# A recurrent gate block with routed experts: tile partitions in four contiguous quarters of 32 batches

## The chip, the cores and the metric

The kernel runs on one core of one Trainium2 chip. The metric is device time in microseconds (us), from the kernel's runs without a profiler.

## The reference, cut to what matters

`x` is 32 batches of 256 time steps of 128 float32 features. Everything below is float32.

```python
xn = layernorm(x, ln_w, ln_b)
u = xn @ Ws.T + bs + xn @ Wi.T + bi              # 16 states
h_t = tanh(h_{t-1} @ A.T + u_t)                  # over the 256 steps, all 32 batches
a = (H @ Wo.T + bo) * sigmoid(xn @ Wg.T + bg) + x
x = layernorm(x + a)
# 8 experts (128 -> 176 -> 128, gated), the two best of each token, plus a shared expert
x = layernorm(x + experts(x) + shared(x))
```

The recurrence is the part that cannot be split over time: each of the 256 steps needs the state of the step before, for 32 batches at once.

## The kernel before, in words

**Tiles.** The 256 steps are cut into 16 tiles of 16 steps. A tile holds 32 batches x 16 steps = 512 tokens, as 128 partitions with 4 tokens each. The 16 steps of a tile are four quarters (`tq`) of four steps (`q`). A partition holds the four steps of one quarter of one batch, 2 KB that lie together in HBM. Before, partition number = 4 x batch + quarter, so that one DMA with the pattern `k b tq (q d)` (lines 232 and 233) loads a tile (`load_x`, L426 to L429) or stores one (L511 to L514).

**From tokens to columns.** The normalized tile `xn` is transposed in four pieces of 128 x 128, one for each `q` (`four_transposes`, L1226 to L1230). Column `q * 128 + partition` of `xnT`, of the PSUM bank `pu` and of the state `hT` is then the token of that `q` and partition. The 32 columns of one time step are what `step_cols` (L388 to L390) returns: before, every fourth column of a block of 128, so with a stride of 16 bytes in float32.

**The recurrence.** One loop counter `n` runs over all engines' programs; step `n` is time step `n` for 0 to 255. In step `n` TensorE adds `A h` of the step before into the 32 columns of `pu` (L1342, a float32 matmul that the profile counts as two weight loads and two matmuls), then ScalarE takes tanh of these columns into `hT` (L656), and TensorE waits for it before the next step. Between two such matmuls TensorE does about one other piece of work, put there by hand by the tables `AT` (line 51), `AT_OWN` and the stages `SPARSE`: the projections of the next tile (L1368, L1371), the gate (L1358, L1361), the output (L1377, L1380), transposes (L1229), router logits (L1401), and the shared expert (L1270, L1275, L1280, L1287, L1288). Where there is little to do, `hold_clock` (L1311 to L1314) adds idle matmuls.

**Experts.** A tile's tokens are scattered by GpSimd (L567) into pages of 256 rows per expert in HBM (`xs`). From step 250 on, pages are loaded by SyncE (SP; L477 for rows, L482 for weights), put through the experts and scattered back by GpSimd (L574) to `ys`. The page phase ends at about 500 us of the profiled execution.

**The final sums.** For each tile, SP loads 512 KB of `ys` (L508), VectorE and, for tiles 6 to 15, TensorE (L1328 to L1330) add the parts, VectorE takes the moments (L779, L785, L793), GpSimd the root (L555), VectorE the shift (L800), ScalarE normalizes (L615), and SP stores the tile (L514). Tiles 0 to 5 are summed within the page phase. `SUM_AT` and `SUM_LAST` (lines 211 to 214) fix the order: for tiles 6 to 15 the steps are 3 apart, the load of a tile comes 5 steps before its sum and its store 9 steps after. So on SP's queue the store of tile i stands just ahead of the load of tile i + 5: store 6, load 11, store 7, load 12, and so on to store 10, load 15, and then stores 11 to 15. There are five buffers for these loads and three for the results.

**SP's queue at the start.** `load_x(0)`, four small weights (L433), `load_x(1)`, three more weights (L437), `load_x(2)`, nine small ones (L441 to L443), `load_x(3)`, `load_x(4)`. Then SP waits for `weights_zeroed` (L446), which VectorE's `other_weights` gives (L749 to L755), and issues 14 loads of expert weights (L449 to L455). VectorE's `expert_biases` (L768) waits for these at step 10, and the output gate of tile 0 (`og`, step 19) is behind it on VectorE. `other_weights` stands on VectorE behind the moments of tiles 0 to 2 (L779) and the shift of tile 2 (L800), for which GpSimd's root (L555) stands behind its `constants` (L534).

**Later loads of x** are issued 56 steps ahead of a tile's first step and used 44 steps ahead of it.

Of the kernel before, what the change touches and what calls it, by code (L numbers as in the profile page):

```python
# [6 lines left out]
def rnn_gate_moe_block(nc, x, Ws, bs, Wi, bi, Wo, bo, Wg, bg, ln_w, ln_b, A,  # L7
# [4 lines left out]
    B, S, D = x.shape  # L12
    N = A.shape[0]
    E, _, H = w1.shape
    P = 128
    STEPS = 16
    TOK = B * STEPS
    Q = TOK // P
    TILES = S // STEPS
# [53 lines left out]
    NX, NW, NH, NY, NT, NE, NL, NG, NS, NP, NB = 10, 7, 3, 5, 5, 8, 5, 3, 3, 3, 4  # L73
# [155 lines left out]
                found += [(b, i) for i in range(2 * Q * len(tiles)) if n == first + int(i / rate)]  # L229
        return found  # L230

    xv = x.rearrange("b (k tq q) d -> k b tq (q d)", tq=STEPS // Q, q=Q)
    ov = out.rearrange("b (k tq q) d -> k b tq (q d)", tq=STEPS // Q, q=Q)

    with ExitStack() as ctx:
        def sb(name, shape, dt=fp32):
# [39 lines left out]
        xt = [sb(f"xt{i}", [P, Q, D]) for i in range(NT)]  # L276
# [56 lines left out]
        yo, yn = xt[0:4], [xt[4], xn, x1r[0]]  # L333
# [19 lines left out]
        x_loaded = [sem(f"x_loaded{i}") for i in range(NT)]  # L353
# [25 lines left out]
        out_stored = [sem(f"out_stored{i}") for i in range(3)]  # L379
# [4 lines left out]
        def wait(eng, s, v):  # L384
            if v > 0:
                eng.wait_ge(s, v)

        def step_cols(t):  # L388
            tq, q = divmod(t, Q)
            return slice(q * P + tq, (q + 1) * P, STEPS // Q)  # L390

        def x1_rows(k, c):
            first = (k % NE) * 2 * Q + c * Q
# [28 lines left out]
        def _(sp):  # L422
# [3 lines left out]
            def load_x(k):  # L426
                if k >= NT:
                    sp.wait_ge(v_ready, k - NT + 1)
                sp.dma_start(xt[k % NT][:, :, :].rearrange("p q d -> p (q d)"), xv[k]).then_inc(x_loaded[k % NT], 16)  # L429

            load_x(0)
            for dst, src in ((ws_t, Ws), (wi_t, Wi), (a_t, A), (wg_t, Wg)):
# [52 lines left out]
            for n in range(BEGIN, END):  # L485
                k = event("load", n)
                if k is not None and k >= NT:
                    load_x(k)
                if n == 14:
                    sp.wait_ge(biases_ready, 1)  # L490
                    sp.wait_ge(weights_loaded, 16 * 14)
                    sp.dma_start(packed.rearrange("e p f -> p e f"), weights[:, 0:E, :]).then_inc(packed_stored, 16)
                    sp.wait_ge(pad_made, 3)
                    sp.dma_start(xs[E * STRIDE:E * STRIDE + PAGE, :].rearrange("(p h) f -> p (h f)", h=HALF),
                                 pad[:, :, :].rearrange("p h f -> p (h f)")).then_inc(pad_stored, 16)
                if n == PAD_AT:
                    pads()
                for _, j, c in [load for load in loads if load[0] == n]:
                    load_page(j, c)
                k = summed(n, "load")  # L500
                if k is not None:
                    if k in (0, SOON):
                        for i in range(NY):
                            last = max(j for j in range(sum(PAGES) if k else EARLY_PAGES) if j % NY == i)
                            sp.wait_ge(y_scattered[i], page_done(last))
                    wait(sp, ysum_ready, k - NL + 1)
                    wait(sp, po_ps, k - NL + 1 - SOON)
                    sp.dma_start(yl[k % NL][:, :, :, :].rearrange("p q c d -> p (q c d)"),  # L508
                                 ys[2 * TOK * k:2 * TOK * (k + 1), :].rearrange("(p r) d -> p (r d)", p=P)).then_inc(yl_loaded[k % NL], 16)
                k = summed(n, "store")  # L510
                if k is not None:  # L511
                    i = k
                    sp.wait_ge(normed["out"], i + 1)
                    sp.dma_start(ov[k], yn[i % 3][:, :, :].rearrange("p q d -> p (q d)")).then_inc(out_stored[i % 3], 16)  # L514
                k = event("second", n)
                if k is not None:
                    sp.wait_ge(normed["mid"], k + 1)
                    sp.dma_start(x1_rows(k, 1), x1_rows(k, 0)).then_inc(second_copied[k % NE], 16)
                    if k >= APART:
                        sp.dma_start(yb[k][:, HALF:Q, :], x1_rows(k, 0)[:, HALF:Q, :]).then_inc(half_kept[k % NE], 16)  # L520
            for i in range(3):
                sp.wait_ge(out_stored[i], 16 * len(range(i, TILES, 3)))

        @block.gpsimd
        def _(g):
# [78 lines left out]
        def _(act):  # L604
# [44 lines left out]
            for n in range(BEGIN, END):  # L649
                if n == at("xnT_out", 0):  # L650
                    act.wait_ge(state_weights_ready, 1)
                if 0 <= n < STEPS * TILES:
                    k, t = divmod(n, STEPS)
                    c = step_cols(t)
                    act.wait_ge(h_ps, n + 1)
                    nc.scalar.activation(hT[k % 2][0:N, c], pu[k % 2][0:N, c], ACT.Tanh, bias=bu[:, 0:1]).then_inc(h_ready, 1)  # L656
                for q in range(Q):
                    k = event("in_norm", n, q)
                    if k is not None:
                        wait(act, xnT_ps, k)  # L660
                        normalize("in", k, lambda q: xt[k % NT][:, q, :], xn, (q,))
                for h in range(2):
                    cols = slice(h * PAGE, (h + 1) * PAGE)
                    k = event("xnT_out", n, h)
                    if k is not None:
                        act.wait_ge(xnT_ps, k + 1)
                        ins = nc.scalar.activation(xnT[k % 2][:, cols], pm[:, cols], ACT.Identity, scale=lnw, bias=lnb)
                        if h:
                            ins.then_inc(xnT_ready, 1)
                    k = event("gate_out", n, h)  # L670
                    if k is not None:
                        act.wait_ge(gate_ps, k + 1)
                        wait(act, og_ready, k - NG + 1)
                        ins = nc.scalar.activation(gth[k % NG][:, cols], pm[:, cols], ACT.Tanh, scale=0.5, bias=bgh[:, 0:1])
                        if h:
                            ins.then_inc(gate_ready, 1)
                    k = event("x1T_out", n, h)
                    if k is not None:
                        act.wait_ge(x1T_ps, k + 1)
                        if k >= NS and h == 0:  # L680
                            act.wait_ge(lg_ps, k - NS + 1)
                            act.wait_ge(wb_ps, SHARED_UNIT[k - NS, 0] + 1)
                        ins = nc.scalar.activation(x1T_half(k, h), transposer(k)[:, cols], ACT.Identity)
                        if h:
                            ins.then_inc(x1T_ready, 1)
                if n == PAD_AT + 1:
                    pads()
                b = group("tanh", n)
                if b is not None:
                    act.wait_ge(route_step, 22 * b + 2)  # L690
                    j = Q * len(GROUPS[b])
                    nc.scalar.activation(ex8["th"][:, 0:j, :], ex8["ls"][:, 0:j, :], ACT.Tanh, scale=0.125).then_inc(th_ready, 1)
                for u, j in pages_at("xT", n):
                    act.wait_ge(xpT_ps, j + 1)
                    if j >= NP:
                        act.wait_ge(wb_ps, UNIT_OF_PAGE[j - NP] + 1)
                    nc.scalar.activation(xpT[j % NP][:, :], pt[:, 0:PAGE], ACT.Identity).then_inc(xpT_ready, 1)  # L697
                for u in units_at(n, "t3a", "t3b", "silu"):
                    if SLOT[u]["t3a"] == n:
                        third_a(u)  # L700
                    if SLOT[u]["t3b"] == n:
                        third_b(u)
                    if SLOT[u]["silu"] == n:
                        silu(u)
                for h in range(2):
                    k = summed(n, f"norm{h}")
                    if k is not None:
                        i = k
                        if h == 0:
                            wait(act, out_stored[i % 3], 16 * (i // 3))  # L710
                        for q in (2 * h, 2 * h + 1):
                            normalize("out", i, lambda q: summed_rows(i, q), yn[i % 3], (q,))

        @block.vector
        def _(v):
# [384 lines left out]
            for n in range(BEGIN, END):  # L1100
# [4 lines left out]
                for h in range(2):  # L1105
                    k = event("in_stats", n, h)
                    if k is not None:
                        v.wait_ge(x_loaded[k % NT], 16 * (k // NT + 1))
                        moments("in", lambda q: xt[k % NT][:, q, :], k, (h,))
                k = event("in_scale", n)  # L1110
                if k is not None:
# [5 lines left out]
                k = event("og", n)  # L1117
# [341 lines left out]
```

## Time and profile before

| | us |
|---|---|
| median of 3 runs | 537.75 (537.72 to 538.87) |
| span of the profiled execution, first to last instruction | 536.5 |
| TensorE busy | 478.4 (89%) |
| VectorE busy | 341.1 (64%) |
| ScalarE busy | 337.4 (63%) |
| GpSimd busy | 305.0 (57%) |
| mean granted TensorE clock | 0.946 |

The profiled execution's own device time is not given beside its span; the median of the unprofiled runs is 1.3 us above the span. A row of a timeline gives start, duration, engine, line, operation, tiles and how many instructions of the kind were merged. PE is TensorE's matmul, PEld its weight load, DVE VectorE, ACT ScalarE, POOL GpSimd; SPq is a DMA that SyncE issues, with the time of the issue, not of the transfer. In brackets stands how long the engine was idle before and what ended that.

### The profile page before, as it was taken

The numbers are of one execution on the slowest core, as the hardware profiler recorded it, in microseconds if no ns is written. First come the engines' busy times: TensorE is split into PE (matmuls) and PEld (weight loads), VectorE is DVE, ScalarE is ACT, GpSimd is POOL, SyncE is SP. The second block draws the span as 40 slices with busy tenths as digits, with TensorE's granted clock in tenths as the row PEclk, the third lists the DMA queues.
The fourth block names the chain that finished last, engine by engine and source line by source line (L and its number), as shares of the span: only waits on it lengthen the run. The fifth ranks groups of instructions, "written<-read, shape, count | busy, mean of one in ns | idle before, by whom it ended". The sixth has DMA issues, their size and how long they took to land.

```text
span 536.5 us, 11146 instructions
## 1 busy us (share of the span) xinstructions
PE 478.4 (89%) x2842; PEld 381.2 (71%) x2842; DVE 341.1 (64%) x1514; ACT 337.4 (63%) x870; POOL 305.0 (57%) x337
## 2 busy tenths in 40 slices
PE   5889999999999999897899857999999999999871
PEld 3657777777777777686788746988888888767530
DVE  5353579797979788746575763445454467667752
ACT  3654777777677776435567524677777777777553
POOL 4000003676766676467377777777657777885331
PEclk9977999999999999759999878899999999999987
DMA  3771112232233222278446476558657888841682
GB/s 107 151 235 56 49 47 63 88 92 87 90 90 91 89 72 74 67 220 231 122 140 188 130 215 202 156 140 246 200 167 214 228 264 270 250 167 62 225 288 78
DMA packets 58228, 79.81 MB, mean 149 GB/s; under 512 B 11182, under 2 KB 37803, under 8 KB 58166
## 3 DMA queue, kind: packets, MB, share of 16 engines
q1 hardware_dynamic: 48940, 61.64, 39.7%
q0 software_dynamic: 8640, 16.93, 9.3%
q8 instruction: 24, 0.39, 0.3%
q10 hardware_dynamic: 586, 0.53, 0.3%
q14 instruction: 38, 0.31, 0.2%
HBM read 47.85 MB, written 25.84 MB: 137 GB/s over the span
## 4 chain that ended last, share of the span: by engine, by line
PE 72%; DVE 10%; issue 5%; ACT 5%; DMA 3%; SPq 2%; ACTq 1%; POOL 1%; DVEq 0%; POOLq 0%
PE pu L1342 13%; PE py L1287 9%; PE p L1270 8%; PE py L1288 7%; PE p L1275 7%; PE ph L1280 7%; PE pt L1424 3%; PE pm L1401 3%; DMA weights<-ys 2%; PE pu L1229 2%; ACT hT L656 2%; PE pm L1358 2%; DVE z L1076 2%; PE pu L1380 1%; PE pu L1377 1%
## 5 line engine op out<-in xcount | busy, mean ns | idle before, releaser
L574 POOL DMA_INDIRECT ys<-yp,xp x142 | 141.4, 996 | 55.8 <-issue 38.4
L567 POOL DMA_INDIRECT xs<-x,place_i x128 | 124.1, 970 | 68.4 <-ACT hT L656 28.1
L656 ACT ACTIVATE hT<-pu,bu 16x32 f32<-16x32 f32 x256 | 78.6, 307 | 78.3 <-PE pu L1342 74.3
L1342 PEld LDWEIGHTS pu<-hT,aT 128*128 128x128 f32 x512 | 81.8, 200 | 58.2 <-ACT hT L656 52.8
L1342 PE MATMUL pu<-hT,aT 128*128 128x32 f32 x512 | 105.7, 293 | 11.6 <-ACT hT L656 11.5
L647 ACT ACTIVATE hid<-z 128x512 f32<-128x512 f32 x103 | 64.7, 628 | 65.3 <-DVE z L1076 63.3
L1071 DVE SCALAR_TENSOR_TENSOR z<-p,wp,t3a 128x256 f32<-128x256 f32 x71 | 34.3, 483 | 78.5 <-ACT t3a L635 68.0
L1287 PE MATMUL py<-wp,hid 128*128 128x128 f32 x284 | 60.4, 295 | 14.2 <-DVE yp L1097 12.0
L1287 PEld LDWEIGHTS py<-wp,hid 128*128 128x128 f32 x284 | 46.0, 196 | 29.8 <-DVE yp L1097 19.9
L555 POOL TENSOR_TENSOR rstd_in<-ve_in,neghalf 128x4 f32<-128x4 f32 x16 | 16.4, 1026 | 73.8 <-DVE ve_in L793 73.7
L1288 PE MATMUL py<-wp,hid 128*128 128x128 f32 x284 | 56.6, 282 | 0.0
L1288 PEld LDWEIGHTS py<-wp,hid 128*128 128x128 f32 x284 | 44.8, 199 | 0.0
L1270 PE MATMUL p<-xpT,wp 128*128 128x256 f32 x142 | 43.6, 390 | 0.0
L1275 PE MATMUL p<-xpT,wp 128*128 128x256 f32 x142 | 43.0, 385 | 0.0
L1280 PE MATMUL ph<-xpT,wp 128*128 128x256 f32 x142 | 42.6, 382 | 0.1
L635 ACT ACTIVATE t3a<-p,wp 128x256 f32<-128x256 f32 x71 | 33.3, 469 | 7.1 <-issue 4.5
L640 ACT ACTIVATE t3b<-ph,wp 48x256 f32<-48x256 f32 x71 | 33.4, 470 | 5.6 <-PE ph L1280 3.7
L1076 DVE SCALAR_TENSOR_TENSOR z<-ph,wp,t3b 48x256 f32<-48x256 f32 x71 | 33.8, 476 | 2.8 <-ACT t3b L640 2.6
L697 ACT ACTIVATE xpT<-pt 128x256 f32<-128x256 f32 x71 | 27.2, 383 | 10.1 <-PE pt L1424 8.7
L1424 PE MATMUL pt<-ident,xp 128*128 128x128 f32 x142 | 28.7, 285 | 3.9 <-issue 2.9
L615 ACT ACTIVATE xn<-xt,shift_in,rstd_in 128x128 f32<-128x128 f32 x64 | 30.3, 478 | 2.4 <-DVE shift_in L800 2.4
L555 POOL TENSOR_TENSOR rstd_out<-ve_out,neghalf 128x4 f32<-128x4 f32 x16 | 17.7, 1107 | 23.8 <-DVE ve_out L793 23.8
(264 smaller groups left out, 984.4 us busy)
## 6 DMA issues: line engine op xcount, KB each, us to landing
wp<-packed SPq DMA_DIRECT2D x71, 320.0 KB, 3.3
xp<-xs SPq DMA_DIRECT2D x71, 130.0 KB, 2.9
weights<-ys SPq DMA_DIRECT2D x16, 512.0 KB, 4.4
xt<-in_L_attn_x SPq DMA_DIRECT2D x16, 256.0 KB, 3.1
x<-x SPq DMA_DIRECT2D x16, 256.0 KB, 2.7
packed<-weights SPq DMA_DIRECT2D x1, 2560.0 KB, 8.6
ys<-yp,xp POOLq DMA_INDIRECT x142, 3.0
yb<-x SPq DMA_DIRECT2D x16, 128.0 KB, 2.8
```

The costliest lines, as they stand in the source:

```text
L567: g.indirect_dma_start(out=xs[:, :], out_offset=bass.IndirectOffsetOnAxis(ap=place_i[b % NB][:, c, t * Q + q:t * Q + q + 1], axis=0), in_= ...
L574: g.indirect_dma_start(out=ys[:, :], out_offset=bass.IndirectOffsetOnAxis(ap=xp[j % NX][:, h, DEST:DEST + 1].bitcast(int32), axis=0), in_= ...
L647: nc.scalar.activation(hid[u % NH][:, :], z[u % 2][:, :], ACT.Silu).then_inc(hid_ready, 1)
L656: nc.scalar.activation(hT[k % 2][0:N, c], pu[k % 2][0:N, c], ACT.Tanh, bias=bu[:, 0:1]).then_inc(h_ready, 1)
L1076: nc.vector.scalar_tensor_tensor(out=z[u % 2][0:REST, PAGE:2 * PAGE], in0=ph[0:REST, 0:PAGE], scalar=packed_of(u)[0:REST, BIAS + 2:BIAS + ...
L1270: nc.tensor.matmul(p3[:, 0:PAGE], w[:, W3A:W3A + P], src, start=True, stop=True).then_inc(w3_ps, 1)
L1275: nc.tensor.matmul(p1[:, 0:PAGE], w[:, W1A:W1A + P], src, start=True, stop=True).then_inc(w1_ps, 1)
L1280: nc.tensor.matmul(ph[:, 0:PAGE], w[:, WB:WB + P], src, start=True, stop=True).then_inc(wb_ps, 1)
L1287: nc.tensor.matmul(o, hid[u % NH][:, h * P:(h + 1) * P], w[:, W2A:W2A + D], start=True, stop=False)
L1288: ins = nc.tensor.matmul(o, hid[u % NH][:, PAGE + h * P:PAGE + (h + 1) * P], w[:, W2B:W2B + D], start=False, stop=True)
L1342: nc.tensor.matmul(pu[k % 2][:, step_cols(t)], aT[:, :], before, start=False, stop=True, skip_group_check=True).then_inc(h_ps, 1)
L1424: ins = nc.tensor.transpose(pt[:, h * P:(h + 1) * P], xp[j % NX][:, h, 0:D], ident[:, :])
```

## The change

A tile's partition number becomes 32 x quarter + batch. The 32 columns of a time step are then contiguous. A load of x and a store of the result become four DMAs of 32 partitions (64 KB) each, on the same semaphores, whose waits count four times as much.

```diff
-    xv = x.rearrange("b (k tq q) d -> k b tq (q d)", tq=STEPS // Q, q=Q)
-    ov = out.rearrange("b (k tq q) d -> k b tq (q d)", tq=STEPS // Q, q=Q)
+    QUARTERS = STEPS // Q
+    xv = x.rearrange("b (k tq q) d -> k tq b (q d)", tq=QUARTERS, q=Q)
+    ov = out.rearrange("b (k tq q) d -> k tq b (q d)", tq=QUARTERS, q=Q)
...
         def step_cols(t):
             tq, q = divmod(t, Q)
-            return slice(q * P + tq, (q + 1) * P, STEPS // Q)
+            return slice(q * P + tq * B, q * P + (tq + 1) * B)
...
             def load_x(k):
                 if k >= NT:
                     sp.wait_ge(v_ready, k - NT + 1)
-                sp.dma_start(xt[k % NT][:, :, :].rearrange("p q d -> p (q d)"), xv[k]).then_inc(x_loaded[k % NT], 16)
+                for tq in range(QUARTERS):
+                    sp.dma_start(xt[k % NT][tq * B:(tq + 1) * B, :, :].rearrange("p q d -> p (q d)"), xv[k, tq]).then_inc(x_loaded[k % NT], 16)
...
                     sp.wait_ge(normed["out"], i + 1)
-                    sp.dma_start(ov[k], yn[i % 3][:, :, :].rearrange("p q d -> p (q d)")).then_inc(out_stored[i % 3], 16)
+                    for tq in range(QUARTERS):
+                        sp.dma_start(ov[k, tq], yn[i % 3][tq * B:(tq + 1) * B, :, :].rearrange("p q d -> p (q d)")).then_inc(out_stored[i % 3], 16)
...
-                sp.wait_ge(out_stored[i], 16 * len(range(i, TILES, 3)))
+                sp.wait_ge(out_stored[i], 16 * QUARTERS * len(range(i, TILES, 3)))
...
-                            wait(act, out_stored[i % 3], 16 * (i // 3))
+                            wait(act, out_stored[i % 3], 16 * QUARTERS * (i // 3))
...
-                        v.wait_ge(x_loaded[k % NT], 16 * (k // NT + 1))
+                        v.wait_ge(x_loaded[k % NT], 16 * QUARTERS * (k // NT + 1))
```

## Rows read from the trace of the kernel before

**Rows 1.** Page: the chain that ended last, shares of the span by line.
```profile
PE pu L1342 13%; PE py L1287 9%; PE p L1270 8%; PE py L1288 7%; PE p L1275 7%; PE ph L1280 7%; PE pt L1424 3%; PE pm L1401 3%; DMA weights<-ys 2%; PE pu L1229 2%; ACT hT L656 2%; PE pm L1358 2%; DVE z L1076 2%; PE pu L1380 1%; PE pu L1377 1%
```

**Rows 2.** Timeline of TensorE and ScalarE, one recurrence step at full clock.
```profile
100.68 0.30 PEld L1342 LDWEIGHTS pu<-hT,aT 128*128 128x128 f32 x2 [0.31 <-ACT hT L656]
...
101.13 0.31 ACT L656 ACTIVATE hT<-pu,bu 16x32 f32<-16x32 f32 x1
...
101.50 0.30 PEld L1342 LDWEIGHTS pu<-hT,aT 128*128 128x128 f32 x2 [0.29 <-ACT hT L656]
```

**Rows 3.** Chain in order of time (start, us, what), 101 to 110 us.
```profile
101.10 0.51 PE pu L1380 x2
...
108.46 0.87 PE pm L1401 x8
```

**Rows 4.** The tanh's line L656: ns minimum/median/maximum, first and last start.
```profile
L656 ACT ACTIVATE hT<-pu,bu x256: 291/308/313, 13.1 to 250.6; 16x32 f32<-16x32 f32 x128
```

**Rows 5.** Timelines: last pair of weight loads, and the reader that waited for it.
```profile
95.54 0.30 PEld L1401 LDWEIGHTS pm<-gwT,x1T 128*128 128x128 f32 x2
...
95.98 0.19 DVE L1158 COPY lg<-pm 128x32 f32<-128x32 f32 x1 [1.29 <-PE pm L1401]
...
50.49 0.25 PEld L1229 LDWEIGHTS pu<-ident,og 128*128 128x128 f32 x2
...
51.02 0.69 DVE L1127 SCALAR_TENSOR_TENSOR x1r<-xt,pu 128x512 f32<-128x512 f32 x1 [1.50 <-PE pu L1229]
```

**Rows 6.** Groups by line and form: busy us, mean ns of one | idle before.
```profile
L674 ACT ACTIVATE gth<-pm,bgh 128x256 f32<-128x256 f32 x32 | 14.3, 448 | 0.0
...
L667 ACT ACTIVATE xnT<-pm,vcol 128x256 f32<-128x256 f32 x32 | 17.3, 543 | 1.7 <-PE pm L1229 1.7
...
L615 ACT ACTIVATE x1r<-pm,shift_out,rstd_out 128x128 f32<-128x128 f32 x3 | 1.2, 453 | 0.6 <-DVE shift_out L800 0.6
...
L902 DVE TENSOR_REDUCE new<-sel 128x8 f32<-128x64 bf16 x8 | 2.1, 266 | 0.3
...
L846 DVE TENSOR_REDUCE row_max<-lg 128x8 f32<-128x64 f32 x8 | 1.7, 212 | 0.0
```

**Rows 7.** Timeline of SP's DMA issues at the start.
```profile
3.08 0.42 SPq L433 DMA_DIRECT2D xpT<-in_L_attn_Wg  x1
...
5.49 0.54 SPq L429 DMA_DIRECT2D xt<-in_L_attn_x  x1
...
8.11 0.27 SPq L441 DMA_DIRECT2D brow<-in_L_ffn_b  x1
...
9.12 1.19 SPq L429 DMA_DIRECT2D xt<-in_L_attn_x  x2
```

**Rows 8.** Chain in order of time at the start.
```profile
0.80 3.25 DMA xt<-in_L_attn_x
...
5.78 1.04 POOL rstd_in L555
...
12.34 1.00 POOL rstd_in L555
...
17.17 0.36 SPq L449
```

**Rows 9.** Timeline of SP's DMA issues in the final sums.
```profile
509.63 0.54 SPq L508 DMA_DIRECT2D weights<-ys  x1
...
517.98 0.55 SPq L514 DMA_DIRECT2D out<-xn  x1
518.62 0.54 SPq L508 DMA_DIRECT2D weights<-ys  x1
...
528.60 0.54 SPq L514 DMA_DIRECT2D out<-x1r  x1
530.02 0.54 SPq L514 DMA_DIRECT2D out<-xt  x1
```

**Rows 10.** Chain in order of time in the final sums.
```profile
518.62 4.39 DMA weights<-ys
```

## The prediction

> **What bounds the kernel now.** I read the chain that ended last first [rows 1]. Its largest single line is L1342, the recurrence's matmul, with 13% of the span; the tanh L656, which alternates with it, is there with 2%. To see which of the two engines sets the pace I went to the timeline of one step [rows 2]. The first weight load of L1342 starts at 100.68 us, the tanh at 101.13, the next weight load at 101.50. So 0.45 us pass from TensorE to ScalarE, 0.31 in the tanh, and about 0.06 to the next load: 0.82 us a step. TensorE's other work in such a step is a pair like L1380 with 0.51 us in the chain [rows 3], and the weight loads of L1342 still wait 0.29 to 0.31 us for the tanh [rows 2]. The step is therefore bound by the round trip and not by TensorE's throughput, except where the eight small matmuls of L1401 (0.87 us, [rows 3]) stand between two steps; there TensorE is late, once in each tile. What shortens the matmul's or the tanh's latency shortens nearly every step. The page phase from about 250 us does not read the 32 columns at all.
>
> The other two places that the change touches are SP's queue at the start and in the final sums. At the start the chain goes from x over the moments and GpSimd's root (12.34 us) to the first load of expert weights (17.17 us) [rows 8]; all that follows waits for these weights. At the end SP stores a tile and only then issues the load of another: the store at 517.98 is followed by the load at 518.62 [rows 9], and that load is in the chain with 4.39 us [rows 10].
>
> **Part 1, the matmul's columns: 0.005 us a step.** No row shows L1342 with contiguous columns, so I bound it by readers that wait for a last pair of matmuls. With 8 contiguous columns (L1401) the reader starts 0.44 us after the pair's first weight load, with 128 contiguous ones (the transposes of L1229) 0.53 us [rows 5]. A straight line between them gives 0.44 + 24/120 x 0.09 = 0.46 us for 32. L1342 takes 0.45 [rows 2]. So the stride of 16 bytes costs the matmul nothing that a row at this resolution shows; at most 0.01, if 32 contiguous columns came out like 8. I take 0.005. By the Trainium skill (Advanced Engine Details and Errata, Memory Cachelines), "Any non-contiguous AP significantly slows down matmuls" where PSUM is concerned, since its lines hold two float32. By that rule this term would be the change's main gain; it gives no figure, and these rows do not agree with it at 32 columns.
>
> **Part 2, the tanh: 0.020 us a step.** It takes 308 ns for 32 strided elements [rows 4]. The same function from PSUM, also with a bias from SBUF, takes 448 ns for 256 contiguous ones (L674). The slope comes from L667 and L615, both with scale and bias: (543 - 453)/128 = 0.70 ns per element. Then 32 contiguous elements would take 448 - 224 x 0.70 = 291 ns [rows 6], 17 ns less than now. A second pair of rows, on VectorE, compares reductions of 64 elements to 8: 212 ns in order (L846), 266 ns with a stride of 16 bytes (L902) [rows 6]: 0.84 ns more for each element, which for 32 would be 27 ns. I take 20. The bounds are 0 (a short instruction may have a fixed length) and about 45 (with a slope of 0.84 ns the contiguous tanh would come to 448 - 188 = 260).
>
> **How many steps gain.** The first 21 steps lie ahead of the wait for the expert weights, and steps 240 to 255 among page work. Of the 219 between, about 14 are bound by L1401 and some 15 by other waits (ranks, VectorE). That leaves 190. Gain: 190 x 0.025 = 4.75 us. TensorE has room for it: 0.51 for the other pair and 0.22 for L1342's (two of the eight that take 0.87 us, [rows 3]) make 0.73 against a step of 0.79.
>
> **Part 3, price of a quarter transfer on SP.** A whole tile's issue takes 0.54 us, and two take 1.19 with the gaps, 0.05 between two issues. The nearest others are 0.42 us (128 rows of 512 B) and 0.27 (8 rows) [rows 7]. None has 32 rows of 2 KB. I take 0.45, as rows of 128 partitions lie on both sides of it, so with the gap 4 x 0.49 = 1.96 us in place of 0.60: 1.36 us more a tile. The bounds are 4 x 0.31 and 4 x 0.60: 0.65 and 1.8 more. By the Trainium skill (DMA: Bandwidth & Descriptors, Rules for kernel authors), two transfers to disjoint halves of the partitions run one behind the other on the same engines, and one of 128 partitions is to be preferred: it speaks against this part, and agrees with putting no gain on the shorter transfers.
>
> **Part 4, the start: +1.8 us.** Tile 2's first quarter is issued at 5.49 + 2 x 1.36 = 8.2, its last at 9.7. Landing of a whole tile took 3.25 us and the way from landing to the root 5.78 - 4.05 = 1.7 [rows 8]; with 2.8 for a quarter's landing the root of tile 2 starts at 14.2 in place of 12.34. SP itself has issued tiles 3 and 4 by 9.12 + 3 x 1.36 + 8 x 0.49 = 17.1 [rows 7], ahead of 17.17 + 1.8, so it adds nothing. Queued behind are 14 weight loads, and VectorE and the gate of tile 0 behind these: the delay goes through. Bounds +0.5 (with 0.31 a quarter only tile 0 is late) and +3.5 (0.60 and 3.25 us landing).
>
> **Part 5, loads in the scan and stores in the page phase: 0.** A load is issued 12 steps (10 us) ahead of its use, and SP is mostly idle; 1.4 us more are covered. If that cover went, each tile would pay up to 1.4. The stores of tiles 0 to 5 fall at or behind the last page loads, with SP idle again.
>
> **Part 6, the final sums: +4.8 us.** The store of tile i stands ahead of the load of tile i + 5, whose sum stands on VectorE ahead of the shift of i + 3 and so of its store: a loop of three tiles. One turn, load 12 to load 15, takes 518.62 - 509.63 = 9.0 us [rows 9]. Every turn now takes 1.36 more. Stores 7 and 10 are in two full turns: 2.7. The turn before (stores 4 and 5) has some slack: 0.5. The last store's last quarter goes out 3 x 0.49 = 1.5 later, and stores 14 and 15 are 1.42 apart [rows 9], closer than 1.96: 0.5 more. A quarter may land 0.4 sooner than a whole tile, as I took it at the start. 2.7 + 0.5 + 1.5 + 0.5 - 0.4 = 4.8. Bounds: 1.8 and 7.4 with the two prices.
>
> **Part 7, nothing.** Other places of tokens in the partitions change neither the number of rows per expert nor the count or size of scatters, pages and waits: 0. The semaphore waits are the same waits with larger numbers: 0.
>
> **Sum.** Against the profiled execution: 1.8 - 4.75 + 4.8 = +1.85 us. Its span of 536.5 stands 1.3 us below the median of the runs, and I carry the difference over: 537.75 + 1.85 = 539.6.
>
> **Rivals.**
> 1. The stride is dearer than these rows say, in the tanh, in the matmul, or both. The point from which it decides is 6.6 / 190 = 0.035 us a step. At 0.055 (45 ns of tanh, 10 of matmul) it gives 10.5 us, and 537.75 + 6.6 - 10.5 = 533.9. For it: 13% of the chain is this line. Against it: 0.45 us is what the two contiguous rows give. Chance 0.16, at 532 to 536.6. The Trainium skill's rule on PSUM lines (Advanced Engine Details and Errata, Memory Cachelines) points here.
> 2. A quarter's issue is cheap, 0.27 us. The costs are then 0.5 + 1.8, and the time 537.75 + 2.3 - 4.75 = 535.3, faster. For it: the row of 8 partitions. Against it: a 128-row issue with short rows is 0.42, so the number of rows is not the whole price. Chance 0.13.
> 3. The change does not do what it says: 32 elements are too few for the stride to matter, the tanh has a fixed length, and only SP's costs are left: 537.75 + 6.6 = 544.4. For it: the tanh's minimum of 291 ns [rows 4] occurs with the stride too. Chance 0.18.
> 4. Gain and costs are alike, within 0.2% (1.1 us), about what a measurement of this kernel can tell from no change. Chance 0.14.
>
> The forecast itself, slower at 538.9 to 544, keeps 0.39. In sum: faster 0.29, same 0.14, slower 0.57. The range from 533.8 to 544.8 leaves out 0.1 on each side; the forecast's own is 538.9 to 544.
>
> **What the changed profile would show.** The tanh's median at 285 to 292 ns in place of 308, and L1342's first load to the tanh still at 0.45 us; steps at 0.79 us. Four x issues of about 0.45 us a tile on SP, and the first load of expert weights at 19 us in place of 17.17. Four stores a tile in the final sums, with load 15 some 3.5 us further from the page phase's end, the last issue 5 us further. Wrong would prove me: a tanh at 308 or under 270, a latency well under 0.44 us in the matmul, or quarters at 0.3 us.

## The result, and the profile after

The changed kernel takes 534.6 us (median; the kernel before beside it 538.0). The ratio, taken over the fast runs alone, is 0.9934, with a 95% interval from 0.9910 to 0.9959: faster by 0.7%, or 3.6 us (2.2 to 4.8). The difference is small, but its interval leaves out 1. The forecast was slower by 1.85 us. The profiled execution went from a span of 536.5 to 531.9 us.

The page of the changed kernel, the chain that ended last by line (L1346 is the recurrence's matmul, L1342 before; lines from the load of x to SP's store are 3 higher than before, all behind the store 4 higher):

```profile
PE pu L1346 11%; PE py L1291 9%; PE p L1274 7%; PE py L1292 7%; PE p L1279 7%; PE ph L1284 7%; PE pt L1428 3%; PE pm L1405 3%; DMA weights<-ys 3%; POOL ys L578 2%; PE pu L1233 2%; PE pm L1362 2%; ACT hT L660 1%; DVE z L1080 1%; PE pu L1384 1%
```

The recurrence's matmul fell from 13 to 11% [rows 1], the loads of the final sums rose from 2 to 3%. The tanh's line, and a timeline of two steps:

```profile
L660 ACT ACTIVATE hT<-pu,bu x256: 262/278/279, 14.0 to 242.6; 16x32 f32<-16x32 f32 x128
```
```profile
100.66 0.30 PEld L1346 LDWEIGHTS pu<-hT,aT 128*128 128x128 f32 x2
...
101.11 0.28 ACT L660 ACTIVATE hT<-pu,bu 16x32 f32<-16x32 f32 x1
101.43 0.30 PEld L1346 LDWEIGHTS pu<-hT,aT 128*128 128x128 f32 x2
...
102.21 0.30 PEld L1346 LDWEIGHTS pu<-hT,aT 128*128 128x128 f32 x2
```

The tanh's median went from 308 [rows 4] to 278 ns. Two steps take 102.21 - 100.66 = 1.55 us, 0.775 each, against 0.82 [rows 2]. By the exact starts the usual distance between two tanhs went from 0.814 to 0.777 us: 37 ns, 30 of them the tanh's own. The other 7 lie between the first weight load of L1342 and the start of the tanh, 0.455 us in the median before and 0.448 after. The last tanh starts at 242.6 us in place of 250.6 [rows 4].

The start, SP's issues and the chain in order of time, and x's row of the page:

```profile
0.80 1.78 SPq L432 DMA_DIRECT2D xt<-in_L_attn_x  x4
...
4.02 0.42 SPq L436 DMA_DIRECT2D xpT<-in_L_attn_Wg  x1
...
7.51 1.70 SPq L432 DMA_DIRECT2D xt<-in_L_attn_x  x4
...
12.14 3.67 SPq L432 DMA_DIRECT2D xt<-in_L_attn_x  x8
```
```profile
4.02 2.04 DMA xpT<-in_L_attn_Wg
...
9.74 1.01 POOL rstd_in L559
...
12.81 0.99 POOL rstd_in L559
...
17.63 0.35 SPq L452
```
```profile
xt<-in_L_attn_x SPq DMA_DIRECT2D x64, 64.0 KB, 2.0
```

The root of tile 2 starts at 12.81 us (12.34 before), the first load of expert weights at 17.63 (17.17) [rows 8]: 0.46 us later.

The final sums, SP's issues (each x4 is one tile's store) and pieces of the chain:

```profile
502.49 1.72 SPq L518 DMA_DIRECT2D out<-xn  x4
504.30 0.37 SPq L511 DMA_DIRECT2D weights<-ys  x1
...
512.52 1.71 SPq L518 DMA_DIRECT2D out<-xn  x4
514.33 0.37 SPq L511 DMA_DIRECT2D weights<-ys  x1
...
525.81 2.13 SPq L518 DMA_DIRECT2D out<-xt  x4
```
```profile
494.17 4.87 DMA weights<-ys
...
504.30 4.77 DMA weights<-ys
...
514.33 4.13 DMA weights<-ys
```

The loop that the prediction describes is now in the chain with three loads (tiles 9, 12 and 15), each behind a store. A turn takes 514.33 - 504.30 = 10.0 us in place of 9.0 [rows 9].

Where the 4.6 us of the two profiled executions lie, by the starts of the first output gate, the last tanh and the first final sum on TensorE (us; the other columns are experiments, told below; the last row is called the last stretch from here on):

| stretch | before | after | columns only | quarters only | hT in step order | the same, late loads first |
|---|---|---|---|---|---|---|
| start to first output gate | 31.8 | 32.3 | 31.8 | 32.2 | 31.8 | 32.1 |
| to the last tanh | 218.7 | 210.3 | 211.8 | 214.6 | 211.7 | 214.2 |
| of it steps 48 to 240 | 162.2 | 157.0 | 157.0 | 162.3 | 157.0 | 157.0 |
| to the first final sum | 249.1 | 249.8 | 246.5 | 249.9 | 250.2 | 249.6 |
| to the end | 36.8 | 39.6 | 37.3 | 40.0 | 37.5 | 32.6 |

So +0.4, -8.4, +0.6 and +2.8. Steps 48 to 240 took 162.2 to 162.3 us in all three profiled kernels whose hT has strided columns, and 156.9 to 157.1 in all eleven in which they are contiguous; the rest of the scan does not repeat so well, because of the clock. The windows from 33 to 58 us, in the kernel before and in the changed one (busy time of the five engines, granted clock, DMA share, GB/s):

```profile
33.00:58.00 25.00, 22.93 (x120) 17.41 (x118) 11.90 (x63) 12.42 (x39) 2.25 (x4) 0.73 0.42 143
```
```profile
33.00:58.00 25.00, 22.68 (x137) 17.59 (x137) 12.93 (x67) 14.08 (x45) 2.25 (x4) 0.86 0.45 148
```

Around the wait for the expert weights TensorE was busy for 3.3, 3.7 and 2.7 of each 4 us from 24 to 36 us before, and for 3.2, 3.8 and 2.6 after. Then the clock fell to 1.2 GHz in both, at 34.6 us for 13.7 us before, and at 36.8 us for 6.8 us after (granted 0.73 and 0.86 of the stretch). Steps 24 to 48 took 24.5 and 21.9 us. Most of that difference is not the change's: with contiguous columns alone they took 24.2 us at 13.7 us of low clock. So about 2.3 of the 8.4 us are this execution's clock.

What ends the span is not the last store. The last instructions of GpSimd and of SP, before and after:

```profile
L235 POOLq DRAIN  x1: 9300/9300/9300, 526.9 to 526.9; - x1
...
L235 SPq DRAIN  x1: 13/13/13, 532.6 to 532.6; - x1
```
```profile
L237 POOLq DRAIN  x1: 9300/9300/9300, 522.4 to 522.4; - x1
...
L237 SPq DRAIN  x1: 7/7/7, 529.4 to 529.4; - x1
```

GpSimd's program ends with a drain that begins with its last root (that of tile 15) and takes 9.30 us. The span ends 0.2 us behind it, 9.50 us from the start of that root. SP, which waits for the landing of the last store, was done 3.6 us earlier before and 2.2 us earlier after. The chain of the profile does not show this: it breaks off at ScalarE's last normalization.

### The profile page after: what moved, and what is told of

The parts are those of the page before. It is cut to its first block, busy times and chain, and to the rows that moved or that the text cites. A ratio compares the mean times of both kernels' runs of the same rounds, so it can differ in the third digit from the quotient of the medians.

```text
span 531.9 us, 11242 instructions
## 1 busy us (share of the span) xinstructions
PE 469.5 (88%) x2842; PEld 379.6 (71%) x2842; DVE 341.1 (64%) x1514; ACT 334.2 (63%) x870; POOL 308.8 (58%) x337
## 4 chain that ended last, share of the span: by engine, by line
PE 67%; DVE 10%; issue 6%; ACT 5%; DMA 4%; SPq 3%; POOL 3%; ACTq 1%; DVEq 0%; POOLq 0%
PE pu L1346 11%; PE py L1291 9%; PE p L1274 7%; PE py L1292 7%; PE p L1279 7%; PE ph L1284 7%; PE pt L1428 3%; PE pm L1405 3%; DMA weights<-ys 3%; POOL ys L578 2%; PE pu L1233 2%; PE pm L1362 2%; ACT hT L660 1%; DVE z L1080 1%; PE pu L1384 1%
## 5 line engine op out<-in xcount | busy, mean ns | idle before, releaser
L578 POOL DMA_INDIRECT ys<-yp,xp x142 | 145.2, 1023 | 55.6 <-issue 36.9
L660 ACT ACTIVATE hT<-pu,bu 16x32 f32<-16x32 f32 x256 | 70.8, 277 | 73.0 <-PE pu L1346 64.0
L1346 PEld LDWEIGHTS pu<-hT,aT 128*128 128x128 f32 x512 | 81.0, 196 | 49.8 <-ACT hT L660 40.9
L1346 PE MATMUL pu<-hT,aT 128*128 128x32 f32 x512 | 101.8, 282 | 10.8 <-ACT hT L660 10.3
L701 ACT ACTIVATE xpT<-pt 128x256 f32<-128x256 f32 x71 | 27.2, 383 | 10.2 <-PE pt L1428 8.8
```

The costliest lines, as they stand in the source:

```text
L578: g.indirect_dma_start(out=ys[:, :], out_offset=bass.IndirectOffsetOnAxis(ap=xp[j % NX][:, h, DEST:DEST + 1].bitcast(int32), axis=0), in_= ...
L1346: nc.tensor.matmul(pu[k % 2][:, step_cols(t)], aT[:, :], before, start=False, stop=True, skip_group_check=True).then_inc(h_ps, 1)
```

## The experiments

**Contiguous columns alone**, on the kernel before:

```diff
-            return slice(q * P + tq, (q + 1) * P, STEPS // Q)
+            return slice(q * P + tq * B, q * P + (tq + 1) * B)
```

> The kernel before with contiguous columns in step_cols alone; x and the result still move in one transfer a tile with the old partition order. So the recurrence joins tokens that do not belong together; every instruction and its size stays. Theory A (two separate effects: columns pay, the quarters on SP's queue cost): tanh 278 ns, steps of 0.777 us in place of 0.814, and since nothing is added on SP, about 8 us faster than before: 530 us, ratio 0.985. Rival B (the gain comes from the new order of tokens or the shorter transfers, the columns only from the tanh's 0.020 us that I forecast): steps 0.79, ratio 0.991 to 0.993 like the changed kernel's.

Measured: 530.6 us, ratio 0.9869 (0.9825 to 0.9914). The tanh is at 278 ns, the step at 0.777. Theory A: the columns are worth 1.3%, 7 us (4.6 to 9.4), more than the whole change. The interval of the ratio just reaches rival B's 0.991; what decides is the step, 0.777 and not 0.79.

**The quarters alone**, the changed kernel with the reverse of that diff:

> The changed kernel with the strided columns put back in step_cols; the recurrence again joins tokens that do not belong together. Theory A: steps of 0.814 us again, SP's quarters at both ends cost 3.5 us: 541.5 us, ratio 1.0065. Rival B (transfers of a quarter land sooner, 2.0 in place of 3.1 us, and cost nothing in sum): ratio 1.000 within 0.2%.

Measured: 541.4 us, ratio 1.0077 (1.0045 to 1.0110). The quarters cost 4.1 us (2.4 to 5.9), against 6.6 in the prediction. Together the two effects give 0.9869 x 1.0077 = 0.9945, and the change measured 0.9934. Rival B of this run, no cost in sum, falls too.

**Which memory's stride costs**, the changed kernel with strided columns on one side only (`strided_cols` is `step_cols` as it was before). For SBUF:

```diff
-                    before = hT[k % 2 if t else 1 - k % 2][:, step_cols((t - 1) % STEPS)]
+                    before = hT[k % 2 if t else 1 - k % 2][:, strided_cols((t - 1) % STEPS)]
...
-                    nc.scalar.activation(hT[k % 2][0:N, c], pu[k % 2][0:N, c], ACT.Tanh, bias=bu[:, 0:1])
+                    nc.scalar.activation(hT[k % 2][0:N, strided_cols(t)], pu[k % 2][0:N, c], ACT.Tanh, bias=bu[:, 0:1])
```

> The changed kernel, but the tanh writes its 32 states to strided columns of hT in SBUF, and the recurrence's matmul reads them strided; PSUM is contiguous for both engines. The output projection then joins tokens that do not belong together. Theory A1 (the tanh's 30 ns are PSUM reads of lines that are used for one element): tanh 278 ns, and first weight load to tanh 0.45 us; Theory A2 (SBUF's strided write is what costs the tanh): tanh 308 ns. Rival B (a short tanh's length depends on both): between.

For PSUM:

```diff
-                    nc.tensor.matmul(pu[k % 2][:, step_cols(t)], aT[:, :], before,
+                    nc.tensor.matmul(pu[k % 2][:, strided_cols(t)], aT[:, :], before,
...
-                    nc.scalar.activation(hT[k % 2][0:N, c], pu[k % 2][0:N, c], ACT.Tanh, bias=bu[:, 0:1])
+                    nc.scalar.activation(hT[k % 2][0:N, c], pu[k % 2][0:N, strided_cols(t)], ACT.Tanh, bias=bu[:, 0:1])
```

> The mirror of the one before: the recurrence's matmul writes, and the tanh reads, strided columns of PSUM; hT in SBUF is contiguous for both. The recurrence joins tokens that do not belong together. Theory A1: tanh 308 ns, last weight load to tanh 346 ns (matmul slower by 7 ns), steps 0.814 us. Theory A2: tanh 278 ns and matmul as in the changed kernel, steps 0.777 us.

The tanh's line, first with SBUF strided, then with PSUM strided:

```profile
L664 ACT ACTIVATE hT<-pu,bu x256: 292/308/313, 13.4 to 252.1; 16x32 f32<-16x32 f32 x128
```
```profile
L664 ACT ACTIVATE hT<-pu,bu x256: 262/278/279, 13.5 to 243.7; 16x32 f32<-16x32 f32 x128
```

With SBUF strided the scan is as before the change: 308 ns, 0.814 us a step, steps 48 to 240 in 162.2 us; one run took 541.9 us (the quarters alone: 541.4). With PSUM strided it is as after it: 278 ns, 0.777, 157.0 us; one run took 536.0 us (the changed kernel: 534.6). The 30 ns are the tanh's strided write to SBUF. The other 7 ns belong to the matmul (first weight load to tanh 0.456 us with SBUF strided, 0.449 with PSUM strided) and go with hT too, which it reads; its PSUM write is ruled out. Theory A2.

**hT in step order, everything else as before.** If PSUM's stride is free, the partitions need not be reordered at all. On the kernel before:

```diff
+        def hT_cols(t):
+            tq, q = divmod(t, Q)
+            return slice(q * P + tq * B, q * P + (tq + 1) * B)
+
+        def by_step(t, lo, hi):
+            return t[:, lo:hi].rearrange("d (q b tq) -> d q tq b", q=(hi - lo) // P, tq=STEPS // Q)
...
-                    nc.scalar.activation(hT[k % 2][0:N, c], pu[k % 2][0:N, c], ACT.Tanh, bias=bu[:, 0:1]).then_inc(h_ready, 1)
+                    nc.scalar.activation(hT[k % 2][0:N, hT_cols(t)], pu[k % 2][0:N, c], ACT.Tanh, bias=bu[:, 0:1]).then_inc(h_ready, 1)
...
-                    before = hT[k % 2 if t else 1 - k % 2][:, step_cols((t - 1) % STEPS)]
+                    before = hT[k % 2 if t else 1 - k % 2][:, hT_cols((t - 1) % STEPS)]
...
-                    nc.tensor.matmul(pu[k % 2][:, 0:PAGE], woT[:, :], hT[k % 2][:, 0:PAGE], start=True, stop=True)
+                    nc.tensor.matmul(by_step(pu[k % 2], 0, PAGE), woT[:, :], hT[k % 2][:, 0:PAGE], start=True, stop=True)
```

(and the same for the second half, and for the zeroed first state).

> The old partition order with its single transfers. Only hT in SBUF is in time-step order: the tanh writes, and the recurrence's matmul reads, contiguous columns there, while PSUM keeps the strided columns for both; the output projection L1377/L1380 writes its 256 columns to PSUM in permuted order, so the output gate sees the old order again. All values are the reference's. Theory A2 (all of the gain is SBUF's contiguous columns, PSUM's stride is free at any size here): steps 0.777 us, L1377/L1380 as long as before (0.51 us a pair in the chain), and nothing on SP, so as the contiguous columns alone: 530 to 531 us, ratio 0.987. Rival B (a permuted PSUM write of 256 columns is slowed, as 32 columns are too few to show it): L1377/L1380 at 0.9 us a pair or more, twice a tile, 16 tiles: up to 13 us slower than A2, ratio 1.00 to 1.01.

Measured: 531.1 us, ratio 0.9875 (0.9840 to 0.9910). It has the full gain of the columns and no cost on SP. The chain of this kernel has the projection with its 256 permuted columns at the time of the contiguous one [rows 3]:

```profile
111.40 0.51 PE pu L1384 x2
```

**One transfer a tile in the changed layout:**

```diff
-                for tq in range(QUARTERS):
-                    sp.dma_start(xt[k % NT][tq * B:(tq + 1) * B, :, :].rearrange("p q d -> p (q d)"), xv[k, tq]).then_inc(x_loaded[k % NT], 16)
+                sp.dma_start(xt[k % NT][:, :, :].rearrange("p q d -> p (q d)"), xv[k]).then_inc(x_loaded[k % NT], 16)
```

and the same for the store.

> The changed kernel with one transfer a tile for x and for the result, the four quarters as the outermost dimension of the pattern in HBM. Theory A (a transfer is spread over as many DMA engines as its outermost dimension allows, here four): landing of x at 6 us or more in place of 3.1, the result's likewise, so that the start is later by 5 us or more and the end by 3: 540 us or more. Rival B (it is spread over the 128 partitions as before): landing 3.1 us, and 530 us.

Measured: 544.7 us in one run, theory A. The start of its chain, a late piece of it, and the loads' row of its page:

```profile
0.80 5.79 DMA xt<-in_L_attn_x
...
518.40 8.08 DMA weights<-ys
```
```profile
weights<-ys SPq DMA_DIRECT2D x16, 512.0 KB, 7.0
```

The first x takes 5.79 us in place of 3.25 [rows 8]. In the final sums the 512 KB loads, whose own pattern is unchanged, take 7.0 us in the median and 8.08 at the end, behind the slow stores. I had expected the start 5 us later and the end 3. The first load of expert weights went out at 19.7 us in place of 17.2, only 2.5 later, and the last stretch is 47.5 us, 10.7 more than before. Of these, 7.7 lie ahead of GpSimd's last root; the other 3.0 come behind it, as here alone of all the profiled kernels the stores landed after GpSimd's drain (SP was done at 542.7 us, the drain at 539.7). The size fits a transfer spread over few DMA engines, but no row shows how many. By the Trainium skill (DMA: Bandwidth & Descriptors, Why a DMA increments its semaphore by 16 and not by 1), a transfer runs on the largest number of engines, at most 16, that divides the slowest dimension of both patterns, here 4; the slower landing agrees. That is why the change moves quarters in four transfers.

**The order of SP's queue.** First all loads of tiles 6 to 15 two steps earlier, ahead of the stores:

```diff
-    SUM_LAST = dict(load=-5,
+    SUM_LAST = dict(load=-7,
```

on the kernel with hT in step order and on the changed kernel.

> The one before, and in the final sums the load of tile i + 5 goes on SP's queue two steps earlier, ahead of the store of tile i. Theory A (the final sums' loop of three tiles runs over SP's order, store ahead of load): the loads no longer wait for ScalarE, TensorE's and VectorE's waits for them (9 us in the kernel before) go, and the 36.8 us from the first final sum to the end shrink by 3 to 6: 525 to 528 us. Rival B (the loads are bound by their own transfers, 4.4 us for 512 KB, which then queue behind each other): within 1 us of the one before.

> The changed kernel with the load of tile i + 5 two steps earlier, ahead of the store of tile i. Theory A (the quarters cost through the loop store, load, sum, store): most of the 3 us that the final sums lost come back, with what the order costs anyhow: the stretch from the first final sum to the end 34 to 36 us in place of 39.6; 529 to 531 us. Rival B (SP's issue time itself is the bound, 1.9 us a store): 38 to 39 us, 533 to 534.

Measured: 537.8 us, ratio 0.9987 (0.9960 to 1.0014), and 538.9 us, ratio 1.0009 (0.9977 to 1.0041). Both are slower than without this edit, and both expectations failed in the total. The last stretch did shrink, to 32.5 and 34.5 us, but the stretch ahead of it grew from 250 to 258 and 261 us. A timeline of VectorE in the first of the two shows it, in the page phase:

```profile
491.47 0.69 DVE L1192 TENSOR_TENSOR xt<-weights 128x512 f32<-128x512 f32 x1 [8.53 <-DMA weights<-ys]
```

Load 6 waits for the last scattered page. Moved up, it stands ahead of the load of tile 5, whose sum blocks VectorE for 8.53 us, and page work is queued behind that. So only the loads of tiles 11 to 15:

```diff
-        found = [k for k in range(TILES) if n == SUM_AT[k] + (SUM_SOON if k < SOON else SUM_LAST).get(what, END)]
+        found = [k for k in range(TILES) if n == SUM_AT[k] + (SUM_SOON if k < SOON else SUM_LAST).get(what, END) - 2 * (what == "load" and k > 10)]
```

> The kernel with the old partition order and hT in step order in SBUF, and of the final loads only those of tiles 11 to 15 go on SP's queue two steps earlier, ahead of the stores of tiles 6 to 10; loads 6 to 10 stay where they are, so that none of them stands ahead of the loads and stores of tiles 0 to 5. Theory A (the order store, load is what the loop of three tiles runs over; the 8.7 us lost before TensorE's first final sum came only from load 6 waiting ahead of tile 5's load): 250 us from the last tanh to the first final sum again, 32.5 to 34 us from there to the end, 527 to 528.5 us, ratio 0.980. Rival B (loads 11 to 15 are then bound by their own transfers): 36 to 37.5 us for the last stretch, 531 us.

> The changed kernel with the same earlier place of loads 11 to 15. Theory A: the last stretch 34 to 35 us in place of 39.6, 529.5 to 531 us, so what is left of the quarters' cost is about 1.5 to 2 us (the last store's four issues and the stores that come closer together than 1.8 us). Rival B (the issues of the quarters bound the stretch themselves): 38 us or more, 533 us.

Measured: 526.8 us, ratio 0.9805 (0.9753 to 0.9856), and 528.0 us, ratio 0.9845 (0.9787 to 0.9904). The last stretch is 32.6 us on the old layout and 35.1 on the new one. The changed kernel gains 0.9934 - 0.9845 = 0.9%, 4.8 us, from the order alone: of its 39.6 us at the end 4.5 lay in the loop. What the quarters still cost there is 35.1 - 32.6 = 2.5 us. The first of the two beats both kernels by a clear margin. The second missed its expectation of the stretch slightly (34 to 35 us, 1.5 to 2 us left), and its reason too: the rest is not the last store's four issues, as the stores are not what ends the span. It was there already at the last load, which went out 16.8 us behind the first final sum with quarters and 13.8 without, and at the last root (25.6 and 23.1).

**Loads or stores in quarters.** The changed kernel with x loaded in one transfer in the old order (`xw`, shown), and the changed kernel with the loads in four but the result stored in one in the old order (not shown):

```diff
-                for tq in range(QUARTERS):
-                    sp.dma_start(xt[k % NT][tq * B:(tq + 1) * B, :, :].rearrange("p q d -> p (q d)"), xv[k, tq]).then_inc(x_loaded[k % NT], 16)
+                sp.dma_start(xt[k % NT][:, :, :].rearrange("p q d -> p (q d)"), xw[k]).then_inc(x_loaded[k % NT], 16)
```

> The changed kernel with contiguous columns and quartered stores, but x loaded by one transfer a tile in the old order (32 batches outermost), so that tokens stand in other partitions than the store takes them from. Theory A (the start costs 0.5 us, the final sums 3): 534 us less 0.5, ratio 0.992. Rival B (the loads cost as much as the stores): ratio 0.990 or less.

> The changed kernel with quartered loads, but the result stored by one transfer a tile in the old order, so that rows are stored to other tokens. Theory A: the start 0.5 us later, nothing in the final sums: 531 to 531.5 us, ratio 0.988, last stretch 37 us. Rival B: ratio 0.993 like the changed kernel's, last stretch 39 us.

Measured: 532.2 us, ratio 0.9919 (0.9882 to 0.9957), and 531.6 us, ratio 0.9888 (0.9830 to 0.9946). The intervals overlap with each other and with the changed kernel's, so the ratios alone do not part the two. The stretches do: with stores in four the first output gate is at 31.5 us and the last stretch is 39.6; with loads in four 32.4 and 37.1. The other profiled kernels agree, the one with the slow transfers set aside. The first load of expert weights goes out at 17.0 to 17.2 us in the six with whole loads of x and at 17.4 to 17.6 in the seven with quarters. With SP's order as it was, the last stretch is 36.8 to 37.5 us in the four with whole stores and 39.4 to 41.4 in the five with quarters. So the loads cost about 0.4 us at the start and the stores 2 to 3 at the end.

## Why the prediction was wrong, point by point

The gain of the columns and the cost of the quarters on SP's queue were both at work, with their signs, and the sum of the two opposed terms changed its sign. What failed is the cost, 6.6 us (Parts 4 and 6) against 4.1 measured: at the start the landing of tile 2 was not what the chain waited for, and at the end the last store, priced with 1.6 us, is not on the path that ends the span. The tanh's gain (Part 2) was also too small, 0.020 us against 0.030. By the timed medians either correction alone would have left the forecast within 0.7 us of no change (-4.75 + 4.1 or -7.0 + 6.6); the measured gain takes both.

- **What bounds the kernel: right.** The step is the round trip between TensorE and ScalarE; the last tanh came 8 us earlier, of which about 2.3 us are the clock, and page phase and end moved with it.
- **Part 1, the matmul, 0.005 us: right in size** (7 ns). Its cause was named wrongly: I weighed the rule on PSUM lines, but the stride that counts is hT's in SBUF. The Trainium skill's rule on PSUM lines (Advanced Engine Details and Errata, Memory Cachelines) is not borne out here: with 32 strided columns, written by TensorE and read by ScalarE, and with 256 permuted ones, no time was lost.
- **Part 2, the tanh, 0.020 us: 0.030 measured,** within the bounds of 0 and 45 ns. Both pairs of rows that I used gave a price too low (17 and 27 ns), and I took a value between them. That the pair on VectorE came within 3 ns is luck: its strided row reads bfloat16 and the other float32 [rows 6], and it is a read that is strided there, while the tanh's cost is in its write.
- **How many steps gain, 190: about right.** Its share, 190 of 219, would be 167 of the 192 steps from 48 to 240. By the starts of the tanhs in the two traces 160 of them became shorter, by 28 to 42 ns, together 6.0 us; 19 stayed as they were. What the prediction did not have is that some become longer: 12, one a tile, by 30 ns, in which the gate's matmul L1358, released by ScalarE's `xnT` (L667), stands ahead of L1342; and one by 0.34 us, in a longer wait for VectorE's `og`. That leaves 5.2 to 5.3 us there. In steps 24 to 48 the columns brought 0.3 us at the same 13.7 us of low clock (24.5 and 24.2). Over the timed runs they brought 7.0 us, with an interval of 4.6 to 9.4 that holds both these 5.6 and my 4.75, so that no more than the size of a step can be called wrong on this side. The page phase of the kernel with the columns alone, 2.6 us shorter than before, is no gain of the columns: with hT in step order, which has the same columns, it was 250.2 us.
- **Part 3, the price of a quarter, 0.49 us with its gap: 0.45 measured** (1.78 us for four). Close. A quarter's landing, which I put at 2.8 us in Part 4, took 2.0.
- **Part 4, the start, +1.8: 0.46 measured.** I had followed tile 2's own transfers alone. Its last quarter was issued at 8.8 us, not 9.7, and with 2.0 us of landing the tile was there when VectorE came to it (10.86 us, without a wait). The chain runs over Wg instead, issued 0.94 us later, then over the root of tile 1, 0.47 us later (9.74 against 9.27), and GpSimd's constants behind it, which were there before and hid the rest.
- **Part 5, nothing hidden uncovered: right.** Loads in the scan cost nothing that shows (steps 48 to 240 with the quarters alone 162.3 us, before 162.2), nor do the stores of tiles 0 to 5 (last tanh to first final sum 249.9 and 249.1 us, within what kernels with whole stores show).
- **Part 6, the final sums, +4.8: 2.8 measured** in the profiled pair. This is the step that failed most. The loop was near: a turn lost 1.0 us, not 1.36, load 15 went out 3.1 us further from the first final sum, where 3.2 (2.7 + 0.5) were forecast, and GpSimd's last root came 2.8 us further from it (30.1 against 27.3). The terms for the last stores, 1.5 + 0.5 - 0.4 = 1.6 us, are real, as the last issue is 4.7 us further out, but hidden: the span ends 9.50 us after the start of the last root, before and after alike, by GpSimd's drain, and the last store still landed ahead of its end. The chain that I read breaks off at ScalarE's last normalization and does not show that drain.
- **The sum.** Forecast +6.6 - 4.75 = +1.85 us. Timed +4.1 (quarters) - 7.0 (columns) = -2.9, and for the change itself -3.6. The result lies in the first rival's range (532 to 536.6) and near the second's 535.3, and neither has the reason for it alone: the step gained 0.037 us, just over the 0.035 from which the stride decides, and the quarters cost less, though not by a cheaper issue. The prediction has no case in which the stride is dearer and the quarters are cheaper together.

## What to carry to other kernels

In a chain that passes between engines at every step, look at the stride in SBUF of the short operands: here 32 float32 at a stride of 16 bytes cost 30 ns in the write of a 278 ns instruction, and the same stride in PSUM nothing. So, for shapes like these, put the awkward order on the PSUM side of a matmul and keep transfers whole, rather than reorder partitions and pay on the DMA queue. Where a queue holds a store ahead of the load that the next results need, move the load ahead, but only past waits that cannot block it. Before pricing a last store, look at every engine's last instruction, also those that the chain leaves out: here GpSimd's last root, not the store, sets the end.

## What the runs showed of the hardware that I had not expected

- PSUM's stride of 16 bytes was free for TensorE's write and ScalarE's read (278 ns and 0.777 us a step with and without it), while the same stride in SBUF cost 30 and 7 ns.
- GpSimd's last instruction is a drain of 9.30 us in all 14 profiled kernels. In 13 of them the span ends 9.50 us after the start of GpSimd's last root, whatever the stores do; in the one with slow stores it ends 12.55 us after. That is why from the last store's issue to the end 6.4 us pass with whole stores (six kernels) and 4.5 to 4.7 with quarters (seven): the quarter is issued later against a fixed end. With the late loads first the last root came 4.9 us earlier behind the first final sum (23.1 and 28.0), and the end with it. What the drain waits for stays open.
- A pattern whose outermost dimension is 4 made not only its own transfer slow (5.79 us for 256 KB) but also the loads behind it (7.0 us in the median, 4.7 in the changed kernel and 4.4 before).
- From 34 to 37 us on the clock stayed at 1.2 GHz for 6.8, 10.2, 13.7 or 17.1 us in different kernels whose work there was alike. Between two single executions with contiguous columns that is worth up to 3.7 us in steps 24 to 48 (21.8 to 25.4 us), as much as the whole change; only the stretches at full clock repeat.
